# A graph layer's kernel: q and k as two more columns of the projection, and its prologue reordered

## The reference: what is computed

```python
h = maximum(layernorm(x), 0)                        # x: (32, 512, 1024), over the last axis
q = einsum('c,bcn->bn', wq, h);  k = einsum('c,bcn->bn', wk, h)
scores = q[:, None, :] + k[:, :, None]
scores = where(scores > 0, scores, 0.01 * scores)
att = softmax(scores, axis=-1)
agg = einsum('bcn,bmn->bcm', h, att)
out = x + relu(einsum('oc,bcm->bom', adj, agg) + bm[None, :, None])   # adj: (512, 512)
```

## Time and profile before

| | |
|---|---|
| Median of three runs | 2088.07 us (2087.71 to 2090.32) |
| Profiled execution: its time, its span | 2090.47 us, 2088.7 us |
| PE busy | 2051.5 us, 98% of the span |
| DVE, ACT, POOL busy | 1674.8 us (80%), 1221.5 us (58%), 379.6 us (18%) |
| HBM traffic | 202.91 MB read, 67.63 MB written, 130 GB/s |

### The profile page before, as it was taken

How to read it: one execution, slowest core, us unless ns; L and a number is a source line. 1 busy time by engine, 2 the same in 40 slices (tenths; PEclk the granted TensorE clock), 3 DMA queues, 4 the chain that set the end, 5 groups by cost and what they waited for, 6 DMA issues and landing times.

```text
span 2088.7 us, 33534 instructions
## 1 busy us (share of the span) xinstructions
PE 2051.5 (98%) x10448; PEld 950.3 (45%) x10448; DVE 1674.8 (80%) x3661; ACT 1221.5 (58%) x1871; POOL 379.6 (18%) x273
## 2 busy tenths in 40 slices
PE   5899999999999999999999999999999999999999
PEld 2344444444444444444444444444444444444444
DVE  7978878778887788887788877888877888778853
ACT  5556656556655566565566555665655665556634
POOL 1012211112111122111121111221111211112212
PEclk9999999999999999999999999999999999999999
DMA  5244433344324444333433234442334432343332
GB/s 195 64 155 142 148 99 123 138 160 141 133 84 136 151 141 146 104 118 137 161 141 133 84 136 151 141 146 105 117 137 161 141 131 86 136 152 141 106 101 76
DMA packets 126395, 271.46 MB, mean 130 GB/s; under 512 B 22624, under 2 KB 23136, under 8 KB 122208
## 3 DMA queue, kind: packets, MB, share of 16 engines
q1 hardware_dynamic: 123904, 269.01, 37.1%
q10 hardware_dynamic: 2400, 1.58, 0.3%
HBM read 202.91 MB, written 67.63 MB: 130 GB/s over the span
## 4 chain that ended last, share of the span: by engine, by line
PE 95%; DVE 3%; DMA 1%; POOL 0%; issue 0%; ACT 0%; POOLq 0%; SPq 0%; DVEq 0%
PE mix L385 21%; PE mix L387 21%; PE mix L386 21%; PE mix L362 10%; PE mix L363 10%; PE mix L364 10%; PE small L325 2%; DVE den_out L728 1%; PE small L334 1%; DMA xs<-in_x_dram 0%; DVE p_ring L749 0%; DVE p_lo L756 0%; DVE v_lo L761 0%; POOL wm_nat L893 0%; DMA den_row<-den_rows 0%
## 5 line engine op out<-in xcount | busy, mean ns | idle before, releaser
L385 PE MATMUL mix<-p_hi,v_hi 128*128 128x512 f16 x2048 | 776.3, 379 | 5.9 <-DVE p_lo L756 5.4
L386 PE MATMUL mix<-p_lo,v_hi 128*128 128x512 f16 x2048 | 776.2, 379 | 0.0
L387 PE MATMUL mix<-p_hi,v_lo 128*128 128x512 f16 x2048 | 776.2, 379 | 0.0
L911 POOL TENSOR_TENSOR res<-res,y 128x512 f32<-128x512 f32 x256 | 370.5, 1447 | 1688.2 <-ACT y L512 1688.2
L749 DVE SCALAR_TENSOR_TENSOR p_ring<-ab_row,cols,p_ring 128x512 f32<-128x512 f32 x512 | 377.1, 748 | 129.7 <-ACT p_ring L491 129.7
L491 ACT ACTIVATE p_ring<-ab_row,cols 128x512 f32<-128x512 f32 x512 | 349.5, 691 | 192.4 <-DMA ab_row<-ab_rows 132.3
L503 ACT ACTIVATE v_hi<-mix 128x512 f16<-128x512 f32 x256 | 152.7, 597 | 444.1 <-PE mix L364 443.5
L728 DVE SCALAR_TENSOR_TENSOR den_out<-den_row,cols 128x512 f32<-128x512 f32 x512 | 393.4, 806 | 1.0 <-DMA den_row<-den_rows 1.0
L362 PE MATMUL mix<-wmT_hi,h_hi 128*128 128x512 f16 x1024 | 389.1, 380 | 0.0
L364 PE MATMUL mix<-wmT_hi,h_lo 128*128 128x512 f16 x1024 | 388.8, 380 | 0.0
L363 PE MATMUL mix<-wmT_lo,h_hi 128*128 128x512 f16 x1024 | 388.8, 380 | 0.0
(11 more groups left out here) (71 smaller groups left out, 838.9 us busy)
## 6 DMA issues: line engine op xcount, KB each, us to landing
res<-in_x_dram SPq DMA_DIRECT2D x256, 256.0 KB, 3.2
out_dram<-res SPq DMA_DIRECT2D x256, 256.0 KB, 2.1
xs<-in_x_dram SPq DMA_DIRECT2D x124, 512.0 KB, 6.5
den_row<-den_rows SPq DMA_DIRECT2D x32, 1024.0 KB, 4.6
ab_row<-ab_rows SPq DMA_DIRECT2D x64, 512.0 KB, 5.0
res<-in_x_dram SPq DMA_DIRECT2D x4, 512.0 KB, 5.0
wm_nat<-in_adj_dram ACTq DMA_DIRECT2D x1, 1024.0 KB, 12.2
den_rows<-cols SPq DMA_DIRECT2D x32, 8.0 KB, 1.6
```

The source lines that it names most:

```text
L385: pe.matmul(ps[:, :], v_hi[:, b[1], nt, chans], p_hi[:, hf, nt, :], start=(nt == 0), stop=False)
L386: pe.matmul(ps[:, :], v_hi[:, b[1], nt, chans], p_lo[:, hf, nt, :], start=False, stop=False)
L387: mm = pe.matmul(ps[:, :], v_lo[:, b[1], nt, chans], p_hi[:, hf, nt, :], start=False, stop=(nt == NT - 1))
L911: pool.tensor_tensor(res[:, k, :], res[:, k, :], y[:, k % 2, :], ALU.add).then_inc(s_add, 1)
```

## The change

q and k are no longer projected apart. wmT_hi and wmT_lo get two more columns in the first of their two halves of 256 outputs, the upper and lower parts of wq and wk, and every v matmul of 512 columns is cut in one of 258 and one of 256 columns, which go to the two banks of a pair. A v tile takes a pair, so there are two in the ring where there were four banks. ACT copies the two columns to qk4 before each v_hi (not for the first batch). The scaling is taken out in `q_head`, which runs at the start of `early`, after the last v tile; the denominators follow behind all tiles of half 1, and SP writes den_rows at the period's start. spread_qmax moves into a unit, transpose_ab from the third to the sixth node tile of unit 5. On ACT relu(7) moves from behind the eighth p_upper of half 0 behind the fourth, and the work on h behind half 1.

In the prologue the absolute sums of wq and wk are made from their columns (ACT, four values per partition) and summed over partitions by a matmul with ones; the broadcast row loads go. DVE scales two of adj's four tiles, POOL the other two; DVE computes the scales right after the first normaliser. The first batch's q and k come from 96 matmuls of two columns (`first_qk`), its tiles 0 and 1 pass by pass as the split operands come (`first_tiles`); likewise tiles 0 and 1 of the second (`second_tiles`). The `normaliser` of batch (1, 0) moves behind half 0 of the first.

```diff
-        wmT_hi = sb("wmT_hi", [P, CT, O], F16)
-        wmT_lo = sb("wmT_lo", [P, CT, O], F16)
+        wmT_hi = sb("wmT_hi", [P, CT, 2, OH + QK], F16)
+        wmT_lo = sb("wmT_lo", [P, CT, 2, OH + QK], F16)
...
+        pair = [ctx.enter_context(nc.psum_tensor(f"pair{i}", [P, 2, 512], F32)) for i in range(2)]
+        mix = [pair[i // 2][:, i % 2, :] for i in range(MIX)]
...
             def period(b, one, two, three):
+                if one:
+                    write_den_rows(nxt(b))
+                    load_den_rows(nxt(b))
                 store(b, 0)
...
-                if two:
-                    write_den_rows(nxt(b, 2))
-                    load_den_rows(nxt(b, 2))
...
+            def weight_sums():
+                pe.wait_ge(s_on, 1)
+                pe.wait_ge(s_abs, 2)
+                pe.matmul(sums_ps, ones[:, :], wqk_part[:, :], start=True, stop=True).then_inc(s_ws, 1)
+
+            def first_qk(nt, lower):
+
+                nodes = slice(nt * P, (nt + 1) * P)
                 for ct in range(CT):
-                    for part, hp in enumerate((h_hi, h_lo)):
-                        for g in range(NQ):
-                            mm = pe.matmul(rows_ps[g * QG:(g + 1) * QG, :], wqk[:, ct, :],
-                                           hp[:, b[1], ct, g * QN:(g + 1) * QN],
-                                           start=(ct == 0 and part == 0), stop=(ct == CT - 1 and part == 1),
-                                           tile_position=(0, g * QG))
+                    w_hi, w_lo = wmT_hi[:, ct, 0, OH:], wmT_lo[:, ct, 0, OH:]
+                    if lower:
+                        mm = pe.matmul(qk_lo_ps[:, nt, :], h_lo[:, 0, ct, nodes], w_hi, start=(ct == 0), stop=(ct == CT - 1))
+                    else:
+                        pe.matmul(qk_ps[:, nt, :], h_hi[:, 0, ct, nodes], w_hi, start=(ct == 0), stop=False)
+                        mm = pe.matmul(qk_ps[:, nt, :], h_hi[:, 0, ct, nodes], w_lo, start=False, stop=(ct == CT - 1))
+                return mm
+
+            def first_pass(nt, ct, h, w, start=False, stop=False):
+                for half in range(2):
+                    mm = pe.matmul(pair[nt % 2][:, half, 0:OH], h[:, 0, ct, nt * P:(nt + 1) * P], w[:, ct, half, 0:OH],
+                                   start=start, stop=stop)
+                return mm
+
+            def first_tiles():
+
+                for ct in range(CT):
+                    pe.wait_ge(s_hhi, ct + 1)
+                    pe.wait_ge(s_wh, ct + 1)
+                    first_pass(0, ct, h_hi, wmT_hi, start=(ct == 0))
+                pe.wait_ge(s_wqk, 2)
+                for nt in range(NT):
+                    mm = first_qk(nt, False)
                 mm.then_inc(s_qk, 1)
-
-            def select_qk(b):
-                pe.wait_ge(s_qc, cnt(b, Q_OPS, 1))
-                for c in range(2):
-                    mm = pe.matmul(qk_ps[:, c, :, :], qk_rows[:, c * P:(c + 1) * P], select[:, :, :],
-                                   start=True, stop=True)
+                for ct in range(CT):
+                    pe.wait_ge(s_wl, ct + 1)
+                    first_pass(0, ct, h_hi, wmT_lo)
+                for ct in range(CT):
+                    first_pass(1, ct, h_hi, wmT_hi, start=(ct == 0))
+                pe.wait_ge(s_hlo, CT)
+                for nt in range(NT):
+                    mm = first_qk(nt, True)
                 mm.then_inc(s_qk, 1)
+                for ct in range(CT):
+                    mm = first_pass(0, ct, h_lo, wmT_hi, stop=(ct == CT - 1))
+                mm.then_inc(s_v, 1)
+                for ct in range(CT):
+                    first_pass(1, ct, h_hi, wmT_lo)
+                spread_qmax(first)
+                for ct in range(CT):
+                    mm = first_pass(1, ct, h_lo, wmT_hi, stop=(ct == CT - 1))
+                mm.then_inc(s_v, 1)
+
...
             def v_tile(b, nt):
 
-                if nt < MIX and at(b, second):
-                    pe.wait_ge(s_vlo[nt % 2], (nt + MIX) // 2 + 1)
-                elif nt < MIX:
-                    wait(pe, s_y[nt % 2], cnt(b, U // 2, (nt + MIX) // 2 + 1 - U))
+
+                if nt == 0:
+                    pe.wait_ge(s_hlo, cnt(b, CT, CT))
+                if nt < 2:
+                    for i in range(2):
+                        wait(pe, s_y[i], cnt(b, U // 2, nt + 3 - U))
                 else:
-                    pe.wait_ge(s_vlo[nt % 2], cnt(b, NT // 2, (nt - MIX) // 2 + 1))
-                ps, nodes = mix[nt % MIX], slice(nt * P, (nt + 1) * P)
+                    pe.wait_ge(s_vlo[nt % 2], cnt(b, NT // 2, nt // 2))
+                ps, nodes = pair[nt % 2], slice(nt * P, (nt + 1) * P)
                 for ct in range(CT):
-                    if nt == 0 and at(b, first):
-                        pe.wait_ge(s_wl, ct + 1)
                     hi, lo = h_hi[:, b[1], ct, nodes], h_lo[:, b[1], ct, nodes]
-                    pe.matmul(ps[:, :], hi, wmT_hi[:, ct, :], start=(ct == 0), stop=False)
-                    pe.matmul(ps[:, :], hi, wmT_lo[:, ct, :], start=False, stop=False)
-                    mm = pe.matmul(ps[:, :], lo, wmT_hi[:, ct, :], start=False, stop=(ct == CT - 1))
+                    for half, cols_of in enumerate((OH + QK, OH)):
+                        pe.matmul(ps[:, half, 0:cols_of], hi, wmT_hi[:, ct, half, 0:cols_of],
+                                  start=(ct == 0), stop=False)
+                    for half, cols_of in enumerate((OH + QK, OH)):
+                        pe.matmul(ps[:, half, 0:cols_of], hi, wmT_lo[:, ct, half, 0:cols_of], start=False, stop=False)
+                    for half, cols_of in enumerate((OH + QK, OH)):
+                        mm = pe.matmul(ps[:, half, 0:cols_of], lo, wmT_hi[:, ct, half, 0:cols_of],
+                                       start=False, stop=(ct == CT - 1))
...
-                    pe.wait_ge(s_vlo[k % 2], cnt(nxt(b), NT // 2, (k + MIX) // 2 + 1))
+                    pe.wait_ge(s_vlo[k // 2], cnt(nxt(b), NT // 2, NT // 2))
...
-                    if one and k == MIX + 1 and nt == 2:
+                    if one and (k, nt) == (MIX + 1, 5 if two else 1):
                         transpose_ab(nxt(b))
+                    if one and (k, nt) == ((1, 2) if at(b, first) else (0, 3)):
+                        spread_qmax(nxt(b))
...
+            weight_sums()
             transposed_weights()
-            pe.wait_ge(s_wqk, 1)
-            project_qk(first)
-            pe.wait_ge(s_sel, 3)
-            select_qk(first)
-            for nt in range(NT):
-                if nt == 1:
-                    spread_qmax(first)
+            first_tiles()
+            for nt in range(2, NT):
                 v_tile(first, nt)
-            project_qk(second)
-            for nt in range(NT):
-                if nt == 1:
-                    select_qk(second)
-                if nt == 2:
-                    spread_qmax(second)
-                if nt == 3:
+            second_tiles()
+            for nt in range(2, NT):
+                if nt == 4:
                     transpose_ab(first)
                 v_tile(second, nt)
...
             def v_upper(b, nt):
+
                 act.wait_ge(s_v, cnt(b, NT, nt + 1))
-                act.activation(v_hi[:, b[1], nt, :], mix[nt % MIX][:, :], ACT.Copy,
+                ps = pair[nt % 2]
+                if not at(b, first):
+                    act.activation(qk4[:, nt, :], ps[:, 0, OH:OH + QK], ACT.Copy)
+                act.activation(v_hi[:, b[1], nt, :].rearrange("p (h o) -> p h o", h=2), ps[:, :, 0:OH], ACT.Copy,
                                scale=1.0 / H_SCALE).then_inc(s_vhi, 1)
...
-                    if two and nt in (0, 3, 7):
-                        h_upper(h, (0, 3, 7).index(nt))
-                    if two and nt in (1, 5):
-                        h_full(h, nt // 4)
-                    if nt in (2, 4, 6):
-                        relu(b, nt // 2 - 1)
+                    if one and nt == 1:
+                        exponentials(nxt(b))
+                    if nt == 5:
+                        relu(b, 0)
                 if two:
+                    h_upper(h, 0)
+                    h_full(h, 0)
+                relu(b, 1)
+                if two:
+                    h_upper(h, 1)
+                    h_full(h, 1)
+                relu(b, 2)
+                if two:
+                    h_upper(h, 2)
                     h_upper(h, 3)
                 relu(b, 3)
                 if two:
...
                             leak(n, nt + 2)
                         if nt == 0:
                             relu(b, 5)
-                        if nt == 4:
+                        if nt == (1 if two else 3):
                             relu(b, 6)
+                        if nt == (3 if two else 5):
+                            relu(b, 7)
+                        if two and nt == 5:
+                            v_upper(h, 0)
...
             def q_head(b):
-                dve.wait_ge(s_qk, cnt(b, 2, 2))
```

(77 more changed lines are left out.)

218 lines of the change are left out of this document (103 added, 115 removed).

## The result

The kernel after the change takes 2078.29 us (median of 5 runs, 2076.9 to 2079.0) against 2088.74 (5 runs, 2087.71 to 2090.32) before: ratio 0.9949, 95% interval 0.9935 to 0.9963. It is 0.5% faster, 10.5 us of the 18 that I forecast. The profiled execution took 2078.29 us, its span 2076.2.

What follows compares the result with a forecast made beforehand. TensorE (PE), busy 98% of the span, bounds the kernel: 2090.5 - 33.3 + 12 + 3 = 2072.2, less 2.4 from profiled execution to median, forecast 2070 us, 0.9% faster, own range 2060 to 2080.

Steps and rivals of the forecast that it cites:

- 33.3 off: PE, steady batches: 1.44 us of project_qk and select_qk removed, 0.33 added by cut matmuls; net 1.11 us, 30 times.
- I take the middle, 0.1096 each, 0.2192 a pair: v tiles: each 512-column matmul becomes a pair costing 0.2192 us, between 0.2166 and 0.223; 0.33 us added per batch.
- The steady stalls: PE's new waits per batch: 0.2 at v tile 2, 0.05 at tile 3, 0.15 at unit 0; 12 us over 30.
- Unit 0's terms: Next batch's unit 0 waits for v_lower 6: done 63.0, wanted 62.94, plus 0.06 hand-over; price taken 0.15 us.
- The chain from the transpose: Unit 5 to v tile 2: transpose at 29.24, first leak 35.5, v_lower(0) done 47.05, tile 2 wanted at 46.91.
- Rival B: ab chain or two-pair ring becomes the bound: waits of 1.0 us per batch or more, up to 2130 us; chance 0.15.
- Rival A: PE never waits and the prologue's short matmuls cost their lower end: 2051 to 2058 us; chance 0.27.
- Rival C: Weight loads of the cut v matmuls are not hidden: 8.9 us more per batch, 2313 us; chance 0.03.
- Rival D: Prologue loses 15 us instead of 3, short matmuls at twice the price and the chain late: 2082 us; chance 0.03.
- The prologue: Before the steady part: last transposes 6 us sooner, but later waits; 3 us lost, between 4 gained and 8 lost.
- The 96 two-column matmuls: Prologue, first batch's q and k: 8 us taken, between nothing and 9, from 0.09 per 8-column select_qk matmul.
- Denominators 13 to 24: Steady part: denominators run 13 to 24 us into the period, row_scales 25, under the 29.24 at which PE asks.

Runs made afterwards that it cites:

- pitch: Kernel after the change with each row of the moving weights padded from 258 to 288 elements (516 to 576 bytes): 2075.99 us.
- ab3: Kernel after the change with transpose_ab moved back from the sixth to the fourth node tile of unit 5: 2077.71 us.
- pool_idle: Kernel after the change with POOL's addition of x cut to one column of each tile: 2085.81 us.
- all_five: Kernel after the change with v_upper(0) before the eighth leak, normaliser split, spread_qmax later, 576-byte weight rows and batch (1,0)'s normaliser earlier: 2061.22 us.

## Why the prediction was partly right

**The sum held, with one term mis-sized.** From the profiled execution before, 2090.47, I forecast 33.3 off, 12 and 3 on. The profiles show, in those terms: pairs cost 0.58 us per batch, not 0.33, so 25.8 off instead of 33.3; waits 0.38 x 30 = 11.4; prologue 2.1 lost, since the third batch's unit 0 starts at 213.96 for 213.55, with two v phases of 0.86 us saved before it. 2090.5 - 25.8 + 11.4 + 2.1 = 2078.2, measured 2078.3. The terms are not as good as that: the waits of the first two periods stand in 11.4 and in 2.1. Without the double count it is 2090.5 + 0.4 - 28 x (0.86 - 0.38) = 2077.5. Of the 8.3 us between my 2070 and the measured 2078.3, 2.4 are what I took off from the profiled execution to the median; after the change the profiled execution is the median. The failed step is "I take the middle, 0.1096 each, 0.2192 a pair": 0.2219 measured, within its upper end of 0.223. The 0.2192 is what `pitch` shows; the change's own layout added the rest. The Trainium skill ("TensorE: Matmul & The Clock Gate", Back-to-back issue gap) gives columns / 2.4 GHz plus 2.5 ns for the distance of two matmuls. Estimated by it, a pair takes 219.2 ns; `pitch` agrees, and the changed layout is 2.7 ns above it. Nothing in the rows before could show it, since all fp16 moving rows there start on multiples of 512 bytes of their tensor.

**The steady stalls** came in at 0.38 for 0.4 us per batch, at other shares: tile 2 0.18 (0.2 forecast), unit 0 0.11 (0.15), tile 3 none (0.05), and spread_qmax 0.10 where I saw 0.1 of cover. That the sum fits is in part luck: the wait that I had missed makes up for those that I had put too high. Unit 0's terms add up to 0.12, not to the 0.15 that I took, and 0.11 was measured. At spread_qmax two things were missing: q_head is done at 1.92 instead of 1.81, 0.46 behind v_lower(7), and PE starts 0.09 after that, a hand-over that I had not counted. The chain from the transpose held within 0.15 us: asked at 29.24, transpose_ab 29.34; leak 35.5, found 35.63; v_lower(0) 47.05, found 47.16. But I put copy_ab right behind the transpose, and it waits for DVE (29.71); that the two come at the same time is chance, and moving the transpose alone does nothing (`ab3`).

**Rival B** did not decide, but its mechanism is real and its slope is shown: an ab row 0.48 us later cost 0.45 per batch (`pool_idle`). Rival A failed on the layout and on three waits; with all of these mended and the prologue (`all_five`) its 2051 to 2058 is still 3 us away. Rival C is excluded by every run: pairs take 0.218 to 0.222, not 0.4. Rival D is out, since the 96 two-column matmuls cost 2.4 us and not 16.

**The prologue** had about the right sum (2.1 lost, 3 forecast; my terms add up to 4.1) and wrong parts, so its sum was luck. The last transpose came at 20.69 (forecast 21). The 96 two-column matmuls cost 2.4 us, not 8: they start 0.025 apart with a full load each, far below the 0.09 of the 8-column fp32 ones, which was the nearest row and not a near one. So tile 1 was done near 32, not 39, and the last p_lo 3.4 us earlier, not 1 later. But the waits behind it took that back: qmax_p 1.4 (1.6 forecast), ab_pad 2.6 (0.5), first v phase 1.7 (2). The denominators there start only at 100.1, behind normaliser and half 1, and three of them are stretched by POOL. "Denominators 13 to 24" failed in the steady part too (26.7), by the same 1.01 us three times.

## What to carry to other kernels

Where a matmul of 512 columns is cut in two, the second start costs about 2.5 ns and the load hides. Rows of the moving operand that stand at an odd distance, as 516 bytes, can cost as much again: pad them and compare the start times. When the bounding engine gets shorter by one per cent, what it waits for next is set by one instruction's place in another engine's queue: read what stands ahead of the late one, and swap it. Before you do, see whether the late one hangs on a chain that starts with the bounding engine itself: then time saved ahead of it comes back as a longer wait. A wait of 0.1 us that recurs per batch is missing from the table of waits; sum it from start times.

## What was not expected of the hardware

- fp16 matmuls of two columns, each with a 128x128 load of its own, start every 0.025 us; those of 256 columns start every 0.11 us in the v tiles.
- Rows of 516 bytes in the moving operand: 0.2219 us a pair; 576 bytes: 0.2192. With 256 columns read from the rows of 516 bytes it is 0.218 in two channel tiles and 0.222 in the other two, so the start counts and not the distance.
- VectorE's loop turn takes 2.9 us where its branch stands 0.15 us ahead of ab_row's load, and 5.1 where it stands 1.2 us behind it.
- A VectorE instruction with two SBUF operands (the denominators) takes 1.75 us instead of 0.74 when it starts during GpSimd's addition, in three of sixteen per batch.
